# Joined edits to a fused attention and quantized-matmul kernel: order of dense groups, softmax reciprocals, and the weights of the first block

## The reference, cut to what matters

```
xn = layernorm(x)                                  # no gain, eps 1e-5
q, k, v = split(xn @ w_in.T)                       # 16 heads of 64
# per head, windows of 512 queries; keys of the window before and of the own one
scores = q k^T / 8 + slope_h * delta               # valid where 0 <= delta <= 512
o = softmax(scores) v
attn = concat_heads(o) @ w_out.T
x_scale = max(max|xn|, 1e-6) / 127                 # per token
x_q = clip(round(xn / x_scale), -128, 127)         # int8
ffn = (x_q @ weight_q.T) * x_scale * weight_scale + bias
out = x + attn + ffn
```

## Time and profile before

| | |
|---|---|
| median of 3 runs | 1654.83 us (1652.48 to 1738.67) |
| the profiled execution's own time | 1654.68 us |
| its span on the slowest core (core 2) | 1653.1 us |
| spans of the 8 cores | 1645.1 to 1653.1 us |
| TensorE matmul busy | 1566.1 us (95%) |
| VectorE busy | 939.6 us (57%) |
| ScalarE busy | 1060.1 us (64%) |
| GpSimd busy | 840.0 us (51%) |
| granted TensorE clock | 0.993 of full |
| moved by DMA | 213.98 MB |

### The profile page before, as it was taken

One profiled execution on the slowest core, in us unless ns is written; L12 is line 12 of the kernel. 1 busy time (PEld: TensorE's weight loads), 2 busy tenths in 40 slices (PEclk: granted clock), 3 DMA queues, 4 the chain that ended last, 5 costly groups with the idle time before them and its releaser, 6 DMA issues.

```text
span 1653.1 us, 29485 instructions; the slowest of 8 cores (1645.1 to 1653.1 us)
## 1 busy us (share of the span) xinstructions
PE 1566.1 (95%) x8568; PEld 749.9 (45%) x8736; DVE 939.6 (57%) x1696; ACT 1060.1 (64%) x2093; POOL 840.0 (51%) x1242
## 2 busy tenths in 40 slices
PE   4859999999999999999999999999999999999998
PEld 2325444454444445444444544445444444544443
DVE  4535646556475655746566564655647566564454
ACT  3546676766746667776665677667775566767662
POOL 5324536445473644536455563645537554563365
PEclk9979999999999999999999999999999999999999
DMA  7784453433545344353445434344354634435232
GB/s 161 185 222 116 124 147 107 128 116 122 147 133 151 115 128 121 113 146 114 128 132 149 142 109 136 113 121 135 109 141 127 173 116 115 141 109 147 78 79 82
DMA packets 208707, 213.98 MB, mean 129 GB/s; under 512 B 139932, under 2 KB 140060, under 8 KB 208040
## 3 DMA queue, kind: packets, MB, share of 16 engines
q1 hardware_dynamic: 205672, 201.60, 42.2%
q0 software_dynamic: 2880, 10.49, 3.5%
HBM read 149.12 MB, written 37.75 MB: 113 GB/s over the span
## 4 chain that ended last, share of the span: by engine, by line
PE 85%; ACT 6%; DMA 4%; issue 3%; DVE 1%; POOL 1%; SPq 0%; ACTq 0%; DVEq 0%; POOLq 0%
PE dn L578 61%; PE ob L822 7%; PE oa L822 7%; PE sc L730 5%; PE sc L753 5%; ACT p L770 4%; DMA wqk<-w 1%; DMA w2bf<-wqk 1%; ACT r L837 1%; ACT r L835 1%; DMA xpre<-x 1%; SPq L160 0%; DVE p L806 0%; POOL xn L462 0%; DMA xnfm<-xn 0%
## 5 line engine op out<-in xcount | busy, mean ns | idle before, releaser
L770 ACT ACTIVATE p<-sc,kbias_sb 128x512 bf16<-128x512 f32 (+3 forms) x1120 | 489.9, 536 | 235.8 <-PE sc L753 158.6
L578 PE MATMUL dn<-xnfm,wqk 128*128 128x512 bf16 x1996 | 477.1, 382 | 14.6 <-DMA xnfm<-xn 9.6
L664 POOL TENSOR_TENSOR u<-u,xres 128x256 f32<-128x256 f32 x240 | 169.9, 729 | 337.8 <-DVE u L681 337.5
L806 DVE TENSOR_TENSOR p<-p,tri_sb 128x512 bf16<-128x512 bf16 (+1 forms) x608 | 251.3, 414 | 146.4 <-ACT p L787 112.5
L578 PEld LDWEIGHTS dn<-xnfm,wqk 128*128 128x128 bf16 x2048 | 192.6, 98 | 244.5 <-issue 34.4
L787 ACT ACTIVATE p<-sc 128x1024 bf16<-128x1024 f32 (+3 forms) x228 | 214.9, 954 | 107.8 <-PE sc L730 105.9
L578 PE MATMUL dn<-wq_sb,xqfm 128*128 128x512 bf16 x1003 | 240.5, 381 | 6.0 <-DMA xqfm<-xq 2.8
L578 PE MATMUL dn<-wout_sb,ofm 128*128 128x512 bf16 x984 | 233.0, 379 | 6.5 <-issue 4.0
L578 PE MATMUL dn<-wv_sb,xnfm 128*128 128x512 bf16 x985 | 237.2, 380 | 2.0
L822 PE MATMUL oa<-p,vst 128*128 128x512 bf16 (+3 forms) x888 | 217.4, 300 | 4.6 <-DVE ofm L848 4.4
L822 PE MATMUL ob<-p,vst 128*128 128x256 bf16 (+3 forms) x896 | 218.7, 300 | 0.4
(11 more groups left out here) (61 smaller groups left out, 1634.4 us busy)
## 6 DMA issues: line engine op xcount, KB each, us to landing
wqk<-w2bf SPq DMA_DIRECT2D x240, 256.0 KB, 3.0
xpre<-x SPq DMA_DIRECT2D x64, 512.0 KB, 4.5
xres<-x SPq DMA_DIRECT2D x64, 512.0 KB, 4.5
out<-u SPq DMA_DIRECT2D x124, 256.0 KB, 2.2
wqk<-w POOLq DMA_DIRECT2D x16, 256.0 KB, 8.7
w2bf<-wqk SPq DMA_DIRECT2D x16, 256.0 KB, 5.5
wv_sb<-wv POOLq DMA_DIRECT2D x2, 1024.0 KB, 11.8
wq_sb<-wq POOLq DMA_DIRECT2D x1, 2048.0 KB, 13.8
```

The costliest lines, as they stand in the source:

```text
L578: tok = P.op("tensor", lambda e, k=k: e.matmul(out=dn[b][:, :], lhsT=lhs(k), rhs=rhs(k), start=(k == 0), stop=(k == n - 1)), waits=(waits ...
L664: a = P.op("gpsimd", lambda e, q=q: e.tensor_tensor(out=u[:, 256 * q:256 * q + 256], in0=u[:, 256 * q:256 * q + 256], in1=buf[:, 512 * hal ...
L770: tok = P.op("scalar", lambda e, c0=c0, c1=c1, hp=hp, o=o: e.activation(out=pbuf[b % NPB][:, 512 * hp + c0:512 * hp + c1], in_=sc[b % 2][: ...
L806: mask_done[b] = P.op("vector", lambda e: e.tensor_tensor(out=pt, in0=pt, in1=m, op=ALU.mult), waits=[exp_done[b], c_tok])
```

## The change

**Tables.** In `PLAN` the four V groups of half 1 move from slots 1 to 4 into slots 1 and 2; F and P of tiles 0 and 1 move behind them (up to (4, 2)). The load, making and transpose of the quantized rows of tiles 2 and 3 move with them (`XR_LOAD`, `XQ_MAKE`, `XQ_TURN`).

**Reciprocals.** For pairs 3, 5 and 7 the product of the last tile moves one step up (`PV_BEAT_ODD`) and `den` from base + 7 to base + 6.

**Value evacuation.** One ScalarE copy of 128x512 takes the place of two of 128x256.

**Block 0.** The 16 K/Q weight tiles of block 0 go to places of their own, inside `wq_sb` and `wout_sb`, and are never written to `w2bf`. Only two loads are issued at the start, once the first tile of x is there; the others follow at set steps of t = -1. The weights of block 1 (numbers 16 to 31) are loaded as float32 too, four of them at (1, 0) of block 0, and written to `w2bf`; loads from `w2bf` begin with number 32. `wq` is loaded at (3, 1) of block 0 once weights 0 to 7 are used, `wout` at (6, 1) once weights 8 to 15 are. Block 0's rows are normalised by one ScalarE activation (`xn_first`), the mean is taken out of x afterwards on GpSimd (`xn_less_mean`), the row maxima of block 0 move into block 0, and block 1's input has tables of its own (`SECOND_...`).

```diff
+PV_BEAT = {0: 4, 1: 4, 2: 5, 3: 5, 4: 6}
+PV_BEAT_ODD = {0: 4, 1: 4, 2: 5, 3: 5, 4: 5}
 PLAN = [
     [("V", 0, 1), ("V", 0, 2), ("V", 0, 3), ("K", 2, 0), ("Q", 2, 0)],
-    [("V", 1, 0), ("F", 0, 0), ("P", 0, 0), ("K", 3, 0), ("Q", 3, 0)],
-    [("V", 1, 1), ("F", 0, 1), ("P", 0, 1), ("K", 4, 0), ("Q", 4, 0)],
-    [("V", 1, 2), ("F", 1, 0), ("P", 1, 0), ("K", 5, 0), ("Q", 5, 0)],
-    [("V", 1, 3), ("F", 1, 1), ("P", 1, 1), ("K", 6, 0), ("Q", 6, 0)],
+    [("V", 1, 0), ("F", 0, 0), ("V", 1, 1), ("K", 3, 0), ("Q", 3, 0)],
+    [("V", 1, 2), ("P", 0, 0), ("V", 1, 3), ("K", 4, 0), ("Q", 4, 0)],
+    [("F", 0, 1), ("P", 0, 1), ("F", 1, 0), ("K", 5, 0), ("Q", 5, 0)],
+    [("P", 1, 0), ("F", 1, 1), ("P", 1, 1), ("K", 6, 0), ("Q", 6, 0)],
...
-XR_LOAD = {(3, 0): 3}
-XQ_MAKE = {(0, 2): 1, (1, 3): 2, (3, 2): 3}
+XR_LOAD = {(3, 3): 3}
+XQ_MAKE = {(0, 2): 1, (1, 3): 2, (4, 2): 3}
-XQ_TURN = {(0, 4): 1, (2, 3): 2, (4, 3): 3}
+XQ_TURN = {(0, 4): 1, (3, 2): 2, (4, 4): 3}
+FIRST_NORM = {(1, 0): 0, (1, 1): 1, (1, 2): 2, (1, 3): 3}
+FIRST_TURN = {(1, 1): 0, (1, 2): 1, (1, 3): 2, (1, 4): 3}
+FIRST_WEIGHTS = {(1, 0): (2, 3), (2, 4): (8, 9, 10, 11, 12, 13, 14, 15)}
+FIRST_MEAN = {(2, 0): 0, (2, 1): 1, (2, 2): 2, (2, 3): 3}
+FIRST_AMAX = {(0, 1): 0, (0, 2): 1, (0, 3): 2, (0, 4): 3}
+FIRST_SCALES = (1, 0)
+SECOND_LOAD = {(0, 3): 0, (0, 4): 1, (2, 3): 2, (3, 0): 3}
+SECOND_STAT = {(1, 4): 0, (2, 1): 1, (3, 3): 2, (4, 1): 3}
+SECOND_NORM = {(2, 0): 0, (2, 2): 1, (3, 4): 2, (4, 2): 3}
+SECOND_AMAX = {(2, 2): 0, (2, 4): 1, (4, 0): 2, (4, 4): 3}
...
+        def wtile(seq):
+            if seq < 16:
+                t_ = wq_sb if seq < 8 else wout_sb
+                return t_[:, 1024 * (seq % 8):1024 * (seq % 8) + 1024]
+            return wqk[seq % 4][:, :]
+        def load_first(seq, waits=()):
+            wqk_ready[seq] = P.dma("gpsimd", wtile(seq), w2h[fc_of(seq)], f"WB{seq}", waits=waits)
         def load_wqk(seq):
-            if seq >= 16 * NT:
+            if not 16 <= seq < 16 * NT:
                 return
             i = seq % 4
-            if seq < 16:
-                waits = wqk_free[i] + ([w2bf_done[seq - 4]] if seq >= 4 else [])
+            if seq < 32:
+                waits = wqk_free[i] + ([w2bf_done[seq - 4]] if seq >= 20 else [])
...
+        def store_wqk(seq):
+            if 16 <= seq < 32:
+                w2bf_done[seq] = P.dma("sync", w2bf[fc_of(seq)], wqk[seq % 4][:, :], f"WS{seq % 4}",
+                                       waits=[wqk_ready[seq]])
-        for seq in range(4):
-            i = seq
-            wqk_ready[seq] = P.dma("gpsimd", wqk[i][:, :], w2h[fc_of(seq)], f"WG{i}")
+        for seq in range(2):
+            load_first(seq, [xpre_ready[(0, 0)]])
...
+        def load_wq():
+            late_w["wq"] = P.dma("gpsimd", wq_sb[:, :], wqh, "WQ", waits=wb_free[0])
+        def load_wout():
+            late_w["wout"] = P.dma("gpsimd", wout_sb[:, :], wouth, "WO", waits=wb_free[1])
...
+        def xn_first(tc):
+            x = xsrc(0, tc)
...
+            ve = P.op("gpsimd", lambda e: e.tensor_scalar(
+                out=veps[tc][:, :], in0=mv[tc][:, 1:2], scalar1=1e-5, scalar2=1.0,
+                op0=ALU.add, op1=ALU.mult), waits=[v])
+            n = P.op("gpsimd", lambda e: e.tensor_scalar(
+                out=negm[0][:, tc:tc + 1], in0=mv[tc][:, 0:1], scalar1=-1.0, scalar2=0.0,
+                op0=ALU.mult, op1=ALU.add))
+            r = P.op("gpsimd", lambda e: e.tensor_tensor(
+                out=rstd[0][:, tc:tc + 1], in0=veps[tc][:, :], in1=mhalf[:, :], op=ALU.pow),
+                waits=[ve, g_half])
+            m = P.op("gpsimd", lambda e: e.tensor_tensor(
+                out=nmr[:, tc:tc + 1], in0=negm[0][:, tc:tc + 1], in1=rstd[0][:, tc:tc + 1], op=ALU.mult),
+                waits=[n, r])
...
+            xn_ready[(0, tc)] = P.op("scalar", lambda e: e.activation(
+                out=xn[tc][:, :], in_=x[:, :], func=AF.Identity, bias=nmr[:, tc:tc + 1],
+                scale=rstd[0][:, tc:tc + 1]), waits=[m])
+        def xn_less_mean(tc):
+            x = xsrc(0, tc)
+            stats[("d", 0, tc)] = P.op("gpsimd", lambda e: e.tensor_scalar(
+                out=x[:, :], in0=x[:, :], scalar1=negm[0][:, tc:tc + 1], scalar2=1.0,
+                op0=ALU.add, op1=ALU.mult), waits=[stats[("n", tc)], xn_ready[(0, tc)]])
...
# group_kq
-            load_wqk(seq + 4)
+            store_wqk(seq + 2)
+            if seq + 4 >= 32:
+                load_wqk(seq + 4)
             def evac():
+                if 20 <= seq + 4 < 32:
+                    load_wqk(seq + 4)
...
# group_v, evac
-                s = P.op("scalar", lambda e: e.copy(out=first, in_=src[:, :, 0, :]), waits=[tok] + old)
-                s2 = P.op("scalar", lambda e: e.copy(out=second, in_=src[:, :, 1, :]))
+                s2 = P.op("scalar", lambda e: e.copy(
+                    out=vdst(t % 2, tc, half), in_=dn[b][:, :].rearrange("p (a h d) -> p a h d", a=4, h=2)),
+                    waits=[tok] + old)
...
-                            den_plan[base + 7] = (tp, pp, tok)
+                            den_plan[base + (6 if pp >= PAIR2 and pp % 2 else 7)] = (tp, pp, tok)
...
+                        if at == (1, 1):
+                            load_wv0()
+                        if at == (1, 4):
+                            for seq in (4, 5):
+                                load_first(seq)
+                            load_wv1()
+                            for seq in (6, 7):
+                                load_first(seq)
+                            set_ones()
...
+                    if t == 0 and at == (1, 0):
+                        for seq in range(16, 20):
+                            load_wqk(seq)
+                    if t == 0 and at == (3, 1):
+                        load_wq()
+                    if t == 0 and at == (6, 1):
+                        load_wout()
```

More of the change, by code:

```diff
@@ L255, in build_nc @@
         mhalf = cut(1, 1)[0]
+        nmr = cut(1, 4)[0]
         def ps(name, cols):
@@ L265, in build_nc @@
         dma_sems = (["TN", "TQ0", "TQ1", "C", "CK", "CI", "CW", "CB", "XS2", "XS3", "WV0", "WV1", "WO", "WQ", "EA", "EB", "FA", "FB"]
-                    + [f"W{i}" for i in range(4)] + [f"WG{i}" for i in range(4)] + [f"WS{i}" for i in range(4)]
+                    + [f"W{i}" for i in range(4)] + [f"WB{i}" for i in range(16)] + [f"WG{i}" for i in range(4)] + [f"WS{i}" for i in range(4)]
                     + [f"XP{i}" for i in range(2)] + [f"XR{i}" for i in range(NXR)]
@@ L295, in vdst @@
             o = ((slot * 4 + tc) * 8 + half * 4) * 192
[L296 to L299, removed]
+            v = vst[:, o:o + 768].rearrange("p (a h d) -> p a h d", a=4, h=3)
+            return v[:, :, 0:3:2, :]
         def rows_of(t, tc):
@@ L418, in set_ones, with load_wv1 @@
             ones_tok.append(P.op("gpsimd", lambda e: e.memset(vones, 1.0)))
-        def load_late_weights():
+        def load_wv1():
             wv_tok.append(P.dma("gpsimd", wv_sb[:, 4096:8192], wvh[1], "WV1"))
[L423 to L429, removed]
+        def load_wq():
+            late_w["wq"] = P.dma("gpsimd", wq_sb[:, :], wqh, "WQ", waits=wb_free[0])
+        def load_wout():
+            late_w["wout"] = P.dma("gpsimd", wout_sb[:, :], wouth, "WO", waits=wb_free[1])
         def xn_load(t, tc):
@@ L584, in group_kq @@
             seq = 16 * t + QK.index((kind, p))
-            i = seq % 4
-            b, tok = group(8, lambda k: wqk[i][:, 128 * k:128 * (k + 1)],
+            w = wtile(seq)
+            b, tok = group(8, lambda k: w[:, 128 * k:128 * (k + 1)],
                            lambda k: xnfm[:, 512 * k:512 * (k + 1)],
                            [wqk_ready[seq], xnfm_ready[t]])
-            wqk_free[i] = [tok]
+            if seq >= 16:
+                wqk_free[seq % 4] = [tok]
+            else:
+                wb_free[seq // 8] = [tok]
             xnfm_free[:] = [tok]
-            load_wqk(seq + 4)
+            store_wqk(seq + 2)
+            if seq + 4 >= 32:
+                load_wqk(seq + 4)
             def evac():
+                if 20 <= seq + 4 < 32:
+                    load_wqk(seq + 4)
                 if p >= PAIR2:
@@ L890, in build_nc @@
                         if j in n_tiles:
-                            beat = b - i + {0: 4, 1: 4, 2: 5, 3: 5, 4: 6}[i]
+                            beat = b - i + (PV_BEAT_ODD if halves and slot % 2 else PV_BEAT)[i]
                             pv_plan.setdefault(beat, []).append((b, t, slot, j, j == n_tiles[-1]))
@@ L899, in build_nc @@
                         xn_turn_dma(t + 1)
-                    if t + 1 == 0 and at in XN_TURN:
-                        xn_turn(t + 1, XN_TURN[at])
+                    if t + 1 == 0 and at in FIRST_TURN:
+                        xn_turn(0, FIRST_TURN[at])
                     load_at, make_at, turn_at = (
@@ new lines, in build_nc @@
+                    if t + 1 == 0:
+                        if at in FIRST_NORM:
```

(20 more changed lines are left out.)

41 lines of the change are left out of this document (13 added, 28 removed).

## The result

The changed kernel takes 1627.86 us (median of 4 runs, 1626.29 to 1628.79), 0.9835 of the time before, interval 0.9814 to 0.9857. That is 27 us off where the forecast had 34.0. The profiled execution took 1628.03 us, 26.65 less than the 1654.68 of before. All ratios and times given here are of executions in which no die ran slower than the other.

The account below looks back on a forecast made before the run. TensorE's work was taken to bound the steady part, leaving its idle time to win, there and before block 1. 17.0 + 16.35 + 0.6 = 34.0 us off 1654.68 gave 1620.7 us, range 1605 to 1637 (0.8).

Parts of the forecast that it names:

- The steady stalls: After 120 us, TensorE's 24 waits of paired scores for ScalarE's exponentials all go: 17.0 us gained, bounds 0 and 17.0.
- The replay: Steady step re-timed with product and reciprocal moved up: exponentials done at 292.0, buffers wanted at 292.1, 0.1 us to spare.
- rival D: Steady part: the exponentials' wait reappears, ScalarE still late for the next paired scores; 17 us more, 1638; chance 0.13.
- The start: Start of kernel: first dense group at 19.6 us, not 27.35, with tile 3 of x there at 12.5.
- T: Time when block 0's last K/Q group ends, put at 80.0 us, bounds 75 and 90.
- Slot 7 of t = -1: 8.7 us: First dense groups, ahead of block 0's slot 0: 8.7 us at 1.73 us a group, ending at 28.3.
- What is late next: Between block 0 and block 1: transposes and `wout` load both start at T and add up, T + 20, bounds T + 8.5 and T + 22.
- Rival B: Before block 1: transposes get through before `wout` is in its stride, or block 0 at its floor; 11.5 us less, 1609; chance 0.2.
- its own line of 1621.7: Whole kernel: the time below which a measurement tells some 2%, 33 us, from no change; chance of faster 0.45.
- the likeliest case: Whole kernel: the forecast itself, 1620.7 us, by itself 1614 to 1628; chance 0.44.
- Rival C: Block 0 stays bound by DMA, x tiles for block 1 late beside 6 MB of queued weights; 10 us more, 1631; chance 0.15.
- Rival E: Slower than before: the product moved up waits for its mask behind VectorE's copies, 48 times; 1688; chance 0.05.

Follow-up runs that it names:

- the edit alone: Kernel before with only the last product and reciprocal of pairs 3, 5 and 7 one step sooner; ratio 0.9872, span 1630.1 us.
- the first pair: Changed kernel with `wout` held until block 1's transposes land, without and with nine idle products: 1614.32 to 1616.94 us against 1611.77 and 1611.91.

## Why the prediction was right or wrong

**The steady stalls: right in kind, slightly short in size.** All 24 went. The forecast was 17.6 us for everything behind block 1's start, and it was 18.0. But the agreement is partly luck: the edit alone gives 22.3, since each stall was worth 0.88 us, not the 0.71 that the waits' row shows. On the slowest cores 4.3 us are given back (2.3 on the mean of the 8). 1.9 us of it are the new waits for `xnfm`, and 1.1 us lie at the end, where TensorE waits, from 1590 us on, 4.7 us

```profile
PE dn L631 <- DMA xqfm<-xq: 2.8, 1, 2.8
PE dn L631 <- DVE u L708: 1.9, 1, 1.9
```

and 3.6 us with the edit alone. The remaining 1.3 us no view names. The wait of 0.6 us for `ofm`, the forecast's term for the end, did go, but the 1.9 us for VectorE's `u` came in its place.

**The cause within it: not told apart.** The replay was worked through with both moves at once and did not ask which did the work. Had it written ScalarE's list down before and after, it would have shown that `den`'s move changes nothing for pairs 3 and 5. The "0.1 us to spare" of rival D was short: with the product moved, the exponentials are done at 285.33 + 3.03 = 288.36 and the next scores start at 288.94, 0.6 us later.

**The start: right within 1.4 us.** 21.0 against 19.6. The transposes of tile 3 at 18.75 say that the rows came a little later; ScalarE's one activation took the place of GpSimd's two passes as costed.

**Block 0: the failed step, first half.** The term that failed is the gain up to block 1's start: 16.35 us were forecast and 8.6 came. It has two halves, T and the seam behind it. T was put at 80.0 and was 85.3. 1.4 us is the start. 2.2 us is the line "Slot 7 of t = -1: 8.7 us": five groups at 1.73, where it took 10.9 (21.0 to 31.9), since the first ones ran at half rate. The earlier trace rows had this in it: 9.61 us for 31 matmuls is 0.31 us each, not 0.216, and the duration was taken from a steady row instead. Slots 0 to 2 took 10.5 and 19.0 as forecast (for slot 0 the forecast's own prices, 5 x 1.73 + 2.16, give 10.8). Slots 3 to 5 took 23.8 instead of 22.2 (1.6). The forecast had 3 x 1.8 = 5.4 us of waits in these, and 6.0 came (61.4 to 86 us), so the waits are only 0.6 of it. TensorE's granted clock was not full here, 0.93 in the mean of the stretch; 7% of 24.6 us is an estimate of up to 1.7 us lost to it, enough for the rest. The row, and the largest waits:

```profile
61.40:86.00 24.60, 18.67 (x95) 7.64 (x95) 17.45 (x36) 15.80 (x33) 6.67 (x11) 0.93 0.48 177
PE sc L812 <- ACT p L829: 2.8, 4, 0.9
PE oa L881 <- DVE p L865: 1.9, 1, 1.9
...
```

**What is late next: the failed step, second half; right in mechanism, 2.4 us short in size.** `wout` and the transposes did start together at T and did add up: T + 22.4 against T + 20, just past the upper bound of T + 22. The group at half clock behind it came as taken (3.48 us, 3.57 before). Rival B (they get through first) is refuted by the 76 packets of q1 in 8 us. What was sized too small is the load of `wout`. Its 12.0 us were the difference of two landings; alone, with the transposes on TensorE, it took 16.1 us from issue to landing (14.1 to 16.2 over the 8 cores). That is longer than either estimate from bytes in the forecast, 6.8 and 11.6. The two do not add up in full, since 16.1 + 8.5 would be 24.6: some of the transposes pass before the load's packets come. The sign for this mechanism was also read a little too strongly: the last line of the earlier trace rows is of 91.1 to 92 us alone, while over all of 80.2 to 92 q1 moved 274 packets beside q0's 416.

**The sum.** Of the 7.7 us missing up to block 1, 5.3 is T and 2.4 the seam. The forecast of 1620.7 sat one us below its own line of 1621.7, so its chance of 0.45 for more than 2% hung on this term. The time was 1627.9, at the upper edge of the likeliest case's own 1614 to 1628 and 1.65% below before; the interval, 0.9814 to 0.9857, keeps clear of no change.

**Terms costed at nothing.** The order of groups (0.9827 against 0.9835) and the wider copies: right. Weights in time in block 0: right, no wait of TensorE there names one, and `wq` held back brought nothing. Rival C's waits of VectorE for x did not come. Rival E did not come: no product waits for a mask between 120 and 1590 us.

## What to carry to other kernels

When an instruction moves to another step, write down the queue of its engine before and after: if it stands between the same neighbours, nothing has moved, and what helps is the input that comes sooner. When a change frees a place at the same moment as it issues something on the path, ask what is loaded into that place: one more wait on a 2 MB load that nobody needs soon was worth 12.6 us, more than the 8.6 us that the whole change had gained up to block 1. Take the durations of a kernel's first operations from its own first rows, not from its steady state.

## What the runs showed of the hardware

**Two DMA queues share by packets, not by bytes.** 74 packets of 16 KB against 76 small ones in 8 us; 608 against 527, of 0.25 KB each, once the large ones were cut to 1.8 KB. Here the transposes beside the large load lost almost all of their share (0.01 MB in 8 us, against 1.71 MB in 10 us alone), and cutting the large one up gave back 0.6 us of 13.

**The first matmuls run at half rate, and the clock's column does not show it.** In the changed kernel, from the first dense group on (columns as above; TensorE's busy time and count come second):

```profile
21.00:25.50 4.50, 4.49 (x11) 1.58 (x12) 0.69 (x1) 0.58 (x1) 4.50 (x4) 1.00 1.00 166
25.50:30.20 4.70, 4.70 (x23) 2.07 (x22) 1.39 (x2) 1.16 (x2) 4.70 (x8) 1.00 1.06 171
```

and in the kernel with the transposes on TensorE and the nine idle products:

```profile
20.30:24.00 3.70, 3.66 (x17) 1.69 (x18) 0.69 (x1) 0.58 (x1) 3.70 (x3) 1.00 0.92 151
```

11 matmuls in 4.49 us are 0.41 us each, 512 columns at the lower level of 1.2 GHz; then 23 in 4.70, 0.204, at 2.4 GHz. With more work ahead of them it is 0.215 us from the start. The column says 1.00 in all three because it counts time without a record as full speed: on this core the trace's first record of the granted clock, at full, begins at 25.7 us, where the durations change. With the nine products it begins at 17.7 us on the core shown above, ahead of the first group at 20.3, and at 23.2 us on the slowest core of the first pair, whose four groups took 7.86 us, between the two. So at the start of a kernel the durations have to be read, not that column.

**Idle products can be worth having.** Nine that nobody reads shortened the first four groups from 9.81 to 7.86 us and from 9.49 to 7.07, and brought the start of block 1 forward by 1.6 and 2.4 us in two versions. The gain of the whole kernel, some 3 us at most, is not settled.
